# A decoder layer on one core: the product of attention weights and V, one key chunk per step instead of all three in one

## The reference, cut to what matters

```python
xn = layer_norm(x, ln_g, ln_b)
cn = layer_norm(context, cln_g, cln_b)
q = (xn @ Wq).reshape(b, n, HEADS, DIM_HEAD).transpose(0, 2, 1, 3) * scale   # 16 heads of 64
k, v = jnp.split(cn @ Wkv, 2, axis=-1)                                        # one K and V for all heads
sim = jnp.einsum('bhid,bjd->bhij', q, k) + mask[:, None, :, :]
attn = jax.nn.softmax(sim, axis=-1)
out = jnp.einsum('bhij,bjd->bhid', attn, v)
out = out.transpose(0, 2, 1, 3).reshape(b, n, INNER) @ Wout
h = xn @ W1
val, gate = jnp.split(h, 2, axis=-1)
out = out + jax.nn.silu(gate) * val @ W2
```

## Time and profile before

| | |
|---|---|
| median of 3 runs | 1969.52 us (1968.82 to 1971.92) |
| the profiled execution, its time | 1975.6 us |
| its span, first to last instruction | 1973.8 us |
| TensorE busy | 1837.2 us, 93% |
| VectorE busy | 1286.5 us, 65% |
| ScalarE busy | 954.8 us, 48% |
| mean granted TensorE clock | 0.968 of full |

### The profile page before, as it was taken

One profiled execution on the slowest core, in us unless ns is written; L12 is line 12 of the kernel. 1 busy time (PEld: TensorE's weight loads), 2 busy tenths in 40 slices (PEclk: granted clock), 3 DMA queues, 4 the chain that ended last, 5 costly groups with the idle time before them and its releaser, 6 DMA issues.

```text
span 1973.8 us, 28647 instructions
## 1 busy us (share of the span) xinstructions
PE 1837.2 (93%) x9696; PEld 1084.9 (55%) x9696; DVE 1286.5 (65%) x3998; ACT 954.8 (48%) x2326; POOL 419.8 (21%) x569
## 2 busy tenths in 40 slices
PE   4589999999998589899999999999999999999997
PEld 2456767667676344455545545545555555555566
DVE  6688888888864366557557647646656755765744
ACT  3353554464331165545545645645654554554542
POOL 4676876867751010000000000000000000000000
PEclk8689999999998779999999999999999999999999
DMA  4000000000000541112111211111111111111100
GB/s 121 1 1 11 10 10 20 11 20 11 1 10 19 146 129 53 45 52 56 45 45 52 61 42 54 52 49 53 48 49 56 48 49 53 52 49 44 39 17 19
DMA packets 63537, 84.01 MB, mean 43 GB/s; under 512 B 5120, under 2 KB 62112, under 8 KB 62496
## 3 DMA queue, kind: packets, MB, share of 16 engines
q1 hardware_dynamic: 62928, 81.72, 14.8%
q10 hardware_dynamic: 464, 0.46, 0.1%
HBM read 74.82 MB, written 7.34 MB: 42 GB/s over the span
## 4 chain that ended last, share of the span: by engine, by line
PE 61%; DVE 3%; ACT 1%; DMA 1%; issue 1%; SPq 0%; DVEq 0%; ACTq 0%
PE x_ps L1351 19%; PE x_ps L1306 9%; PE x_ps L1313 9%; PE x_ps L1344 9%; PE x_ps L1329 8%; PE x_ps L1420 2%; PE x_ps L1456 1%; PE x_ps L1405 1%; PE x_ps L1413 1%; DMA x_mk<-in_mask 1%; PE x_ps L1426 1%; PE x_ps L1492 1%; DVE x_bn L1042 1%; PE x_ps L1358 1%; DVE x_pr L1697 1%
## 5 line engine op out<-in xcount | busy, mean ns | idle before, releaser
L1697 DVE CUSTOM_DVE_ANT_0 x_pr<-x_ps,x_mk 128x375 f32<-128x375 f32 x448 | 228.1, 546 | 321.3 <-issue 203.8
L1566 ACT ACTIVATE x_pT<-x_ps 125x384 f32<-125x384 f32 x448 | 196.0, 490 | 253.0 <-PE x_ps L1313 251.6
L1572 ACT ACTIVATE x_pr<-x_pr,x_mx 128x375 f32<-128x375 f32 x448 | 268.3, 608 | 33.5 <-DVE x_mx L1697 33.4
L1313 PEld LDWEIGHTS x_ps<-ident,x_pr 128*125 128x125 f32 x1344 | 166.2, 189 | 132.1 <-issue 97.3
L1306 PE MATMUL x_ps<-x_kT,x_qT 64*128 64x375 f32 x896 | 206.9, 537 | 25.2 <-DVE x_mx L1697 20.0
L1313 PE MATMUL x_ps<-ident,x_pr 128*125 128x128 f32 x1344 | 209.0, 292 | 0.8 <-DVE x_pr L1706 0.5
L1351 PE MATMUL x_ps<-x_xn,x_w 128*128 128x448 f32 x512 | 203.9, 541 | 0.0
L1706 DVE TENSOR_SCALAR x_pr<-x_pr,x_rc 128x375 f32<-128x375 f32 x448 | 166.9, 415 | 8.0
L1329 PE MATMUL x_ps<-x_pT,x_va 125*64 125x512 f32 (+1 forms) x768 | 160.4, 553 | 0.6 <-ACT x_pT L1566 0.6
L262 PE MATMUL m_ps<-m_xa,w_in 128*128 128x448 f32 x352 | 147.5, 566 | 5.7 <-ACT m_xa L470 5.7
L1306 PEld LDWEIGHTS x_ps<-x_kT,x_qT 64*128 64x128 f32 x896 | 69.6, 188 | 146.1 <-issue 114.7
(11 more groups left out here) (188 smaller groups left out, 2996.9 us busy)
## 6 DMA issues: line engine op xcount, KB each, us to landing
x_mk<-in_mask SPq DMA_DIRECT2D x224, 187.5 KB, 2.4
x_cx<-in_context SPq DMA_DIRECT2D x32, 375.0 KB
x_mixed<-m_x SPq DMA_DIRECT2D x8, 448.0 KB, 3.2
X<-x_mixed SPq DMA_DIRECT2D x8, 448.0 KB, 4.1
m_X<-in_x SPq DMA_DIRECT2D x7, 448.0 KB, 3.9
out<-f_so SPq DMA_DIRECT2D x7, 448.0 KB, 3.4
fc<-in_fc SPq DMA_DIRECT2D x2, 1024.0 KB, 12.8
x_w<-in_x_w SPq DMA_DIRECT2D x1, 2048.0 KB, 18.6
```

Source lines behind the costliest of these rows:

```text
L1313: last = pe.transpose(bank(2 + e)[0:JP, t * ROWS:(t + 1) * ROWS], pr[:, 2 * (p % SLOT) + e, t * JP:(t + 1) * JP], ident[:, :])
L1566: act.activation(pT[:, 2 * NV * (batch(p) % 2) + 2 * (p % NP % NV) + e, :, :].rearrange("p t s -> p (t s)"), bank(2 + e)[0:JP, 0:JT * ROWS ...
L1572: act.activation(pr[:, k, :], pr[:, k, :], ACT.Exp, scale=-1.0, bias=mx[:, k:k + 1], accum_out=sums[:, k:k + 1]).then_inc(h_e.sem, 1)
L1697: dve.tensor_tensor_reduce(pr[:, k + e, :], bank(e)[:, 0:J], mk[:, p % SLOT, :], -1.0, 3.0e38, ALU.add, ALU.min, mx[:, k + e:k + e + 1]).t ...
```

## The change

`times_v` now does the chunks t0 to t1 of a part instead of all three, and a new `due_v` says in which step each stands. A part h = 0 has its first chunk at r = 6 of its own sequence, and the second and third at r = 0 and r = 1 of the next one. A part h = 1 has its chunks at r = 3, 4 and 5 of the next sequence, except for the last sequence of a group, whose part h = 1 is done whole at r = 2 of the next group's first sequence. ScalarE's `heads_out` moves with the last chunk: to r = 1 and r = 5 (r = 2 in a group's first sequence). Within a step the order stays as it was. After the last group, the second and third chunk of the last h = 0 and the whole of the last h = 1 follow.

```diff
-            def times_v(i, p):
-                b, r = divmod(p, NP)
-                if r not in (NV - 1, NP - 1):
-                    return
-                pe.wait_ge(h_c.sem, h_c.value(i, 2 * p + 2))
-                if r == NV - 1:
-                    emptied(pe, made_in(i, b), ("vback", b))
-                    hold(pe, o_c, i, 2 * b)
-                else:
-                    pe.wait_ge(o_c.sem, o_c.value(i, 2 * b + 1))
-                n, k = r % NV + 1, 2 * NV * (batch(p) % 2)
-                for t in range(JT):
+            def times_v(i, b, h, t0, t1):
+                if t0 == 0:
+                    pe.wait_ge(h_c.sem, h_c.value(i, 2 * (NP * b + (NV, NP)[h])))
+                    if h == 0:
+                        emptied(pe, made_in(i, b), ("vback", b))
+                    hold(pe, o_c, i, 2 * b + h)
+                n, k = (NV, NP - NV)[h], 2 * NV * h
+                for t in range(t0, t1):
...
-                last.then_inc(h_o.sem, 1)
+                if t1 == JT:
+                    last.then_inc(h_o.sem, 1)
+
+            def due_v(i, p):
+
+                b, r = divmod(p, NP)
+                if r == NP - 1:
+                    times_v(i, b, 0, 0, 1)
+                elif b == 0 and i == 0:
+                    return
+                elif r < 2:
+                    times_v(*seq_back(i, b), 0, r + 1, r + 2)
+                elif b == 0 and r == 2:
+                    times_v(*seq_back(i, b), 1, 0, JT)
+                elif b > 0 and r >= 3:
+                    times_v(i, b - 1, 1, r - 3, r - 2)
...
             def group(it, first=False, last=False):
                 for p in range(STEPS):
                     scores(it, p)
-                    if p >= 3 or not first:
-                        times_v(*back(it, p, 3))
+                    due_v(it, p)
...
-            times_v(NG - 1, STEPS - 3)
+            times_v(NG - 1, GB - 1, 0, 1, JT)
             turn(NG - 1, STEPS - 2)
             end_out(1, 1, 0, KH)
-            times_v(NG - 1, STEPS - 2)
             turn(NG - 1, STEPS - 1)
-            times_v(NG - 1, STEPS - 1)
+            times_v(NG - 1, GB - 1, 1, 0, JT)
...
+            def due_heads(i, p):
                 b, r = divmod(p, NP)
...
+                if b == 0 and i == 0:
+                    return
+                if r == 1:
+                    heads_out(*seq_back(i, b), 0)
+                elif r == (2 if b == 0 else 5):
+                    heads_out(*seq_back(i, b), 1)
```

More of the change, by code:

```diff
@@ L1191, in back, with seq_back @@
             return (i, p - n) if p >= n else (i - 1, p - n + STEPS)
+        def seq_back(i, b):
+            return (i, b - 1) if b > 0 else (i - 1, GB - 1)
         def batch(p):
@@ L1572, in exps, with heads_out @@
                     act.activation(pr[:, k, :], pr[:, k, :], ACT.Exp, scale=-1.0, bias=mx[:, k:k + 1], accum_out=sums[:, k:k + 1]).then_inc(h_e.sem, 1)
-            def heads_out(i, p):
-                b, r = divmod(p, NP)
[L1577 to L1582, removed]
+            def heads_out(i, b, h):
+                if h == 0 and b == 0 and i >= 2:
+                    filled(act, i - 1, ("out", KD - 1, 3))
+                at, n = ((0, NV * ROWS), (NV * ROWS, (NP - NV) * ROWS))[h]
+                act.wait_ge(h_o.sem, h_o.value(i, NB * b + h + 1))
+                act.activation(OT[:, i % 2, b, at:at + n], bank(4)[:, 0:n], ACT.Copy).then_inc(o_c.sem, 1)
+            def due_heads(i, p):
+                b, r = divmod(p, NP)
+                if b == 0 and i == 0:
[4 more added lines that the diff above has]
+                    heads_out(*seq_back(i, b), 1)
             def part(it, piece):
@@ L1636, in group @@
                 for p in range(STEPS):
-                    if p >= 3 or not first:
-                        heads_out(*back(it, p, 3))
+                    due_heads(it, p)
                     if p >= 2 or not first:
@@ L1671, in _ @@
             group(NG - 1, last=True)
+            heads_out(NG - 1, GB - 1, 0)
             for p in (STEPS - 2, STEPS - 1):
-                heads_out(NG - 1, p - 1)
                 copies(NG - 1, p)
-            heads_out(NG - 1, STEPS - 1)
+            heads_out(NG - 1, GB - 1, 1)
             end_turned(0)
```

## The result

The changed kernel takes 1978.28 us (median of 6, 1976.25 to 1981.14), the kernel before in the same runs 1970.72. The ratio is 1.0039, with a 95% interval of 1.0024 to 1.0053: about 7.6 us slower (4.7 to 10.4 by the interval), where +6.0 was forecast. The profiled execution took 1981.14 us, 5.5 more than the 1975.6 of the one before.

A forecast was written before the change was run, and what follows sets the result against it. TensorE was taken as the bound; +15.5 us for added bursts, less 2.3, 4.8, 0.35 and 2.0 us of waits, gave +6.0 us: 1975.6 us against the median 1969.52, 0.3% slower, range 1970.0 to 1982.0.

The forecast's parts named there:

- The price of a burst: On TensorE, 111 added product bursts at a fixed 0.14 us each would cost +15.5 us.
- The waits that were to go: Groups 1 to 7: waits filled before step 1 (-2.3 us) and step 27 (-4.8, last group -0.35); 0.68 before step 0 stays.
- Group 0: In the first group, chunks would fill waits before steps 9 and 23 and in step 26: -2.0 us, ends 0 and 5.9.
- My 1.4 us in step 23: In group 0, at most 1.4 us won when the product leaves step 23, until VectorE's maxima end.
- The end: Last group's step 27: transposes start about 4.8 instead of 6.53 us behind the scores; nothing beyond the burst already counted.
- Faster, by bursts without a price: Rival for the added bursts: the fixed 0.14 us is not paid, 15.5 us less, 1960.1 us; chance 0.08.
- No change: Rival: group 0 gives all its 5.9 us and avoided lower clock another 2 us, 1969.6 us; chance 0.15.
- A late copy of the bank: Rival, much slower: ScalarE late with the product's bank in steps 20 and 27, 14 us more, 1989.6 us; chance 0.07.

The follow-up runs named there:

- h = 1 run: The changed kernel with only the parts h = 1 in three steps, the parts h = 0 whole at r = 6: 1976.18 us, 1.0023 to the kernel before.
- h = 0 run: The changed kernel with only the parts h = 0 in three steps, the parts h = 1 whole at r = 2: 1974.87 us, 1.0019 to the kernel before.

## Why the prediction was right, and where it was off

- **The price of a burst** was 0.14 us from the rows of before, and the chunks measured 0.79 and 1.01 us. In groups 1 to 6, where everything else is still, 14 bursts and two waits were to give 14 x 0.14 - 0.33 - 0.79 = +0.84 us; it was +0.77. TensorE was the bound, scores and turn kept their 0.83 and 0.76 us, and the added bursts are nearly all of the loss: that mechanism was right. What I did not see is about 0.15 us gained in step 25, which grew by 0.64 us where a chunk is 0.79.
- **The waits that were to go** went as said: 1.09 to 0.29, 0.33 to none, 0.68 unchanged. The wait of 0.35 us at the end went too.
- **Group 0** is the term that was mis-sized. I had -2.0 us of waits filled, which with 12 added bursts (+1.7) and 1.7 us handed on to group 1 made the group 2 us shorter. Against the trace of the kernel before, steps 6 to 27 are 0.3 us longer, but that trace was at the lower clock for part of them. Against the run with group 0 as before, which hands on the same two chunks, they are 3.6 us longer: 1.7 of bursts, and 1.9 of waits and clock where I had -2.0. The medians put it at about 2 us instead of 3.6, and the intervals of the two ratios allow all from -1 to 5. I had said that steps 9 and 23 lose their product and get a wait instead, and priced this with what was left over. The h = 1 run shows that it is the larger effect: it loses 4.8 to 6.4 us, by which trace it is measured from, through waits of 2 us and the lower clock behind them, where h = 0 alone gains 2.3 to 3.9.
- **My 1.4 us in step 23** was read as a wait that the emptied step would give back. In the run with group 0 as before, step 23 keeps its product and is 1.1 us shorter than in the trace of the kernel before, by the clock alone. So most of that term was a property of the one execution that I read.
- **The end** was to cost nothing beyond its burst. The transposes started 4.81 us behind the last scores, where I had said 4.8. The stretch came 1.4 us shorter than in the profile before, since the clock did not fall there; against the h = 1 run, with the old order at full clock, it is 0.35 us longer.
- **The number** is near for another reason than that all its parts were right. The burst price, which makes up most of it, held; group 0 was missed by 2 to 4 us, in the direction in which the median, +7.6, lies above the forecast. The profiled sum (+5.5) is nearer to the forecast, but by luck: the execution of the kernel before had the lower clock in group 0 and at the end.
- **The rivals.** Faster, by bursts without a price, is excluded by the chunks' own 0.79 and 1.01 us and by the run with chunks split in one step. No change would have needed group 0 to give 5.9 us of waits; it gave none. A late copy of the bank did not occur: no chunk in steps 20 or 27 has a wait.

## What to carry to other kernels

Where TensorE is full, count how often it changes its tiling (row halves, column halves, full width) along its list, and treat each change as 0.15 us of work; splitting a burst to fill gaps pays only where the gap is longer than that. Look at the gaps one by one and move a whole burst into each, before cutting bursts for all of them: here two moved bursts per group won 7 us where 111 new ones lost 8. And before a term is read from one trace, look whether the clock was down there: the same steps took 6.57 and 5.46 us in two executions. Last, ask of each emptied step what its work was covering.

## What the runs showed of the hardware that I had not expected

- The price belongs to the change of form, not to the burst: 0.17 us for each of three and of four added changes in a step, 0.19 for product to full-width matmuls, 0.14 for the product between scores and turn. A turn of three transposes between two chunks takes 0.52 us instead of 0.38.
- A wait costs more than the idle time printed. In the run with the product at the step's end, TensorE took 1288.81 - 1285.31 = 3.50 us for eight records, of which 0.23 was idle; eight such records and a change to the scores take 3.10 us elsewhere. A record is drawn with 0.54 us where the next starts 0.38 us after it when nothing is waited for (1287.67 and 1288.05 in that trace), so a gap hides some 0.16 us more.
- In group 0 the granted clock stood at half behind waits of 1.3 and 2.25 us with only 1.7 us of work between them, and stayed full in the h = 0 run, which has neither wait. It is not the wait alone that decides: behind the 2.05 us at the end the clock fell in the profiled execution of the kernel before and stayed full in that of the h = 1 run, and the scores behind the 3.4 us before step 23 took 1.62 us in one execution and 0.90 in another.
